# Random features of four strips in one call over four PSUM banks, with all five queues reordered, in a two-layer attention and feed-forward kernel

## What is computed

```python
# 1: linear attention by random features, 16 heads of 8, 32 features, causal
q = x_normed * 128**-0.25;  k = ctx * 128**-0.25
q' = exp(q @ R) + 1e-4
k' = exp(k @ R - 0.5*sum(k*k) - max_over_everything(-0.5*sum(k*k))) + 1e-4
x = x + tanh(g) * (causal sum of q'.k' v) / (causal sum of q'.k')
# 2: token-shifted feed-forward: r = sigmoid(xr @ Wr.T); k = relu(xk @ Wk.T)**2
x = x + tanh(g) * r * (k @ Wv.T)
# 3: attention of ctx (queries) over layernorm(x) (keys, values), softmax twice
a = softmax(q @ k.T * s);  gate = 0.5*mean(g) + 0.5*max(g)   # g = normed @ w_la
a = w * softmax(gate * a) + (1 - w) * a
x = x + tanh(g) * ((a @ v) @ w_proj + b)
# 4: quantized SwiGLU: rows to 8 bits by their largest value, weights to -1, 0, 1
x = x + tanh(g) * bitlinear(silu(bitlinear(x, w_gate)) * bitlinear(x, w_up), w_down)
```

## Time and profile before

| | |
|---|---|
| median of 3 runs | 507.24 us |
| all runs | 501.98, 507.24, 509.07 us |
| the profiled execution | 502.71 us |
| its span, first to last instruction | 501.0 us |
| TensorE matmul busy | 457.8 us (91%) |
| VectorE busy | 412.7 us (82%) |
| ScalarE busy | 367.7 us (73%) |
| GpSimd busy | 303.1 us (60%) |

### The profile page before, as it was taken

How to read it: one execution, slowest core, us unless ns; L and a number is a source line. 1 busy time by engine, 2 the same in 40 slices (tenths; PEclk the granted TensorE clock), 3 DMA queues, 4 the chain that set the end, 5 groups by cost and what they waited for, 6 DMA issues and landing times.

```text
span 501.0 us, 19011 instructions
## 1 busy us (share of the span) xinstructions
PE 457.8 (91%) x7616; PEld 336.0 (67%) x7616; DVE 412.7 (82%) x1374; ACT 367.7 (73%) x774; POOL 303.1 (60%) x416
## 2 busy tenths in 40 slices
PE   6678899999999999999999999999999999876864
PEld 2266568777868686868777777778686868554631
DVE  4752666999989898989898989999998989988734
ACT  4455565979797978797878878797979797776542
POOL 6142357576767585858575776767676758384520
PEclk9996979999999999999999999999999999999888
DMA  6401010101101010101010101010010100000000
GB/s 218 120 4 42 6 40 4 40 7 22 34 13 44 11 48 10 47 9 49 7 50 7 51 6 50 6 29 28 19 39 11 46 11 15 9 15 8 6 12 10
DMA packets 31526, 15.15 MB, mean 30 GB/s; under 512 B 12496, under 2 KB 30800, under 8 KB 31440
## 3 DMA queue, kind: packets, MB, share of 16 engines
q1 hardware_dynamic: 31296, 13.92, 10.4%
q10 hardware_dynamic: 144, 0.02, 0.0%
HBM read 9.73 MB, written 2.10 MB: 24 GB/s over the span
## 4 chain that ended last, share of the span: by engine, by line
PE 67%; DVE 18%; issue 6%; ACT 3%; DMA 2%; SPq 2%; POOL 1%; DVEq 0%
PE MC L1548 13%; PE TP L1513 10%; PE FP L1424 7%; PE MA L1440 6%; PE SP L1504 4%; PE SP L1616 4%; DVE SL L1043 3%; DVE emn L1049 3%; PE FP L1403 2%; PE MA L1469 2%; PE SP L1488 2%; PE FP L1360 2%; PE FP L1407 2%; PE FP L1363 2%; PE FP L1405 2%
## 5 line engine op out<-in xcount | busy, mean ns | idle before, releaser
L1548 PEld LDWEIGHTS MC<-Vc,ET 128*64 128x64 f32 x2048 | 65.0, 138 | 22.1 <-issue 19.4
L1548 PE MATMUL MC<-Vc,ET 128*64 128x25 f32 x2048 | 71.6, 218 | 2.1 <-DVE X L1157 1.2
L413 POOL TENSOR_SCALAR ft<-ft 128x512 f32<-128x512 f32 x64 | 39.7, 620 | 52.2 <-ACT ft L634 48.5
L436 POOL TENSOR_TENSOR Zn<-E,rsh 128x1024 f32<-128x1024 f32 x32 | 60.9, 1904 | 11.4 <-DVE rsh L1057 10.1
L444 POOL TENSOR_TENSOR Zn<-Zn,Gs 128x1024 f32<-128x1024 f32 x32 | 60.9, 1904 | 2.7 <-DVE Gs L1067 2.6
L681 ACT ACTIVATE ET<-TP 128x512 f32<-128x512 f32 x64 | 36.5, 597 | 29.3 <-PE TP L1513 29.3
L997 DVE TENSOR_TENSOR WT<-FP,mask 128x512 f32<-128x512 f32 x64 | 41.9, 676 | 10.2 <-PE FP L1424 10.2
L1037 DVE TENSOR_REDUCE mx<-SP 128x16 f32<-128x1024 f32 x32 | 39.0, 1218 | 4.9 <-PE SP L1504 4.8
L675 ACT ACTIVATE ET<-TP 128x512 f32<-128x512 f32 x64 | 37.6, 587 | 6.8 <-PE TP L1513 5.6
L1513 PE MATMUL TP<-ident,E 128*128 128x128 f32 x256 | 39.7, 289 | 1.1 <-ACT E L670 0.9
L1424 PE MATMUL FP<-ft 32*64 32x64 f32 x2048 | 37.9, 223 | 2.3 <-DVE WT L997 1.9
(11 more groups left out here) (211 smaller groups left out, 1179.1 us busy)
## 6 DMA issues: line engine op xcount, KB each, us to landing
Cd<-in_ctx SPq DMA_DIRECT2D x32, 128.0 KB, 3.0
kX<-kT SPq DMA_DIRECT2D x256, 8.0 KB
X<-in_x SPq DMA_DIRECT2D x16, 128.0 KB, 2.7
call<-in_ctx SPq DMA_DIRECT2D x4, 512.0 KB, 6.5
out_x<-X SPq DMA_DIRECT2D x16, 128.0 KB, 2.1
wffn<-in_L_ffn_w_gate SPq DMA_DIRECT2D x1, 256.0 KB, 4.6
wffn<-in_L_ffn_w_up SPq DMA_DIRECT2D x1, 256.0 KB, 4.9
wffn<-in_L_ffn_w_down SPq DMA_DIRECT2D x1, 256.0 KB, 7.1
```

What stands on the lines that cost most here:

```text
L413: pool.tensor_scalar(f, f, EPS_K, 1.0, ALU.add, ALU.mult).then_inc(s("ftp"), 1)
L436: pool.tensor_tensor(z, E1[u][:, :].rearrange("p (h m) -> p h m", m=64), rsh[u][:, :].unsqueeze(2).to_broadcast([P, H, 64]), ALU.subtract) ...
L1548: last = mm(MC[64 * j:64 * j + 64, c + 32 * q:c + 32 * q + 25], weights[:, q, 64 * j:64 * j + 64], Vc[g.p][:, 2 * u + j, q, 0:25], start=T ...
```

## The change

`features` becomes one call for four strips, over the two banks of FP and the two of SP. It is held until the last `less` of the round's stage c has read the scores, and `ffn_gu`, `rows_CT`, `queries` and `scores`, which use SP, are held until the exponentials have read it. With it the five orders are new, as are the waits that go with them:

```diff
-            def features(g, w):
+            def features(g):
                 at_ends(pe, g, s("WT"), g.k * 4)
-                if w == 0:
-                    at(pe, s("Vc"), g.k * 2)
-                    at(pe, s("csq"), g.k + 1)
-                    at(pe, s("kT"), g.k)
-                    at(pe, s("qcT"), g.k + 1)
-                elif w == 1:
-                    at_ends(pe, g, s("Vc"), g.k * 2)
-                    at_ends(pe, g, s("kT"), g.k)
-                    if not g.first:
-                        at(pe, s("fe"), g.k * 4 + 2)
-                bank = SP_ if g.first and w == 1 else FP
-                strips = [(32 * i, 512 * (i % 2), i) for i in (2 * w, 2 * w + 1)]
-                for r, o, i in strips:
+                at(pe, s("Vc"), g.k * 2)
+                at(pe, s("csq"), g.k + 1)
+                at(pe, s("kT"), g.k)
+                at(pe, s("qcT"), g.k + 1)
+                at(pe, s("ls"), g.k * 2 - 2)
+                strips = [(32 * i, (FP, SP_)[i // 2], 512 * (i % 2), i) for i in range(4)]
+                for r, bank, o, i in strips:
                     mm(bank[:, o:o + 256], Rf[r:r + 32, i, :], qcT[r:r + 32, 0:256], start=True, stop=True)
...
# ScalarE
             def features(g, w):
-                at(act, s("f"), g.k * 2 + 1 + w)
-                f = (SP_ if g.first and w == 1 else FP)[:, :].rearrange("p (i t n) -> p t i n", i=2, t=2)
+                if w == 0:
+                    at(act, s("f"), g.k + 1)
+                f = (FP, SP_)[w][:, :].rearrange("p (i t n) -> p t i n", i=2, t=2)
# VectorE
-                v.tensor_tensor(rsh[u][:, :], emn[u][:, :], pos[g.p][:, u, :], ALU.max).then_inc(s("rsh"), 1)
+                v.scalar_tensor_tensor(rsh[u][:, :], emn[u][:, :], 1.0, pos[g.p][:, u, :], ALU.mult, ALU.max).then_inc(s("rsh"), 1)
-                v.tensor_tensor(Gs[u][:, :], gate[g.p][:, u, :], rs1[u][:, :], ALU.mult).then_inc(s("Gs"), 1)
+                v.scalar_tensor_tensor(Gs[u][:, :], gate[g.p][:, u, :], 1.0, rs1[u][:, :], ALU.mult, ALU.mult).then_inc(s("Gs"), 1)
-                    v.wait_ge(s("css"), i + 1)
-                    v.tensor_reduce(cmins[:, i:i + 1], css[:, H * r:H * r + H * n], op=ALU.min, axis=AX.X)\
-                        .then_inc(s("cmins"), 1)
-                v.wait_ge(s("cmins"), 5)
-                v.tensor_reduce(cmin[:, :], cmins[:, :], op=ALU.min, axis=AX.X).then_inc(s("cmin"), 1)
+                v.wait_ge(s("css"), 5)
+                v.tensor_reduce(cmin[:, :], css[:, :], op=ALU.min, axis=AX.X).then_inc(s("cmin"), 1)
```

More of the change, by code:

```diff
@@ L533, in prepare @@
             def prepare():
-                squares(0)
-                squares(1)
+                for i in range(5):
+                    squares(i)
+                masks()
                 act.wait_ge(s("wv_in"), 32)
@@ L724, in step @@
                 if e:
-                    quant_mul(e)
-                if d:
-                    softmax1(d, 2)
-                if e:
                     ffn_in(e)
-                if b:
-                    if b.first:
-                        round_weights()
-                    gates_Tb(b)
                 if d:
@@ L743, in step @@
                 if c:
+                    if c.first:
+                        weights_turned()
                     yC(c)
+                if d:
+                    softmax2(d, 1)
+                if c:
+                    queries_in(c)
+                if e:
+                    ffn_scale(e, 0)
+                if b:
+                    keys(b)
+                if c:
+                    queries(c)
+                if d:
+                    softmax2(d, 2)
                 if a:
+                    if a.k == 1:
+                        scale_weights()
                     yA(a)
                 if d:
-                    softmax2(d, 2)
-                if c:
-                    queries_in(c)
-                if d:
                     softmax2(d, 3)
-                if b:
-                    keys(b)
                 if e:
-                    ffn_scale(e, 0)
+                    ffn_scale(e, 1)
+                    ffn_mid(e, 0)
                 if a:
@@ L759, in step @@
                 if c:
-                    queries(c)
+                    gates_Tb(c)
+                if b:
+                    values1(b)
+                    if b.first:
+                        round_weights()
+                    yB(b)
                 if a:
                     squares_T(a)
-                if b:
-                    values1(b)
-                if e:
-                    ffn_scale(e, 1)
                 if d:
                     attended(d)
+                if c:
+                    softmax1n(c, 0)
                 if b:
-                    yB(b)
+                    if b.first:
+                        wait_setup()
+                    shift_rows(b)
+                if e:
+                    ffn_mid(e, 1)
+                if c:
+                    softmax1n(c, 1)
                 if a:
                     if a.first:
-                        masks()
                         prepare()
                     features(a, 0)
-                if e:
-                    ffn_mid(e, 0)
-                if b:
-                    shift_rows(b)
-                if c:
-                    softmax1n(c, 0)
-                if a:
                     features(a, 1)
@@ L1266, in step @@
                 if b:
+                    if b.first:
+                        weights_clipped()
                     token_mix(b)
@@ L1645, in step @@
             def step(a, b, c, d, e):
[L1646 to L1649 removed]
                 if d:
+                    if d.k == NG - 1:
+                        warm_end(2)
                     outA(d, 0)
[L1652 to L1657 removed]
                 if e:
@@ L1664, in step @@
                 if b:
-                    out0(b, 0)
+                    if b.first:
+                        weights_total()
+                        warm(2)
+                    if b.k == 1:
+                        warm(2)
+                    weights0(b, 1)
                 if e:
@@ L1684, in step @@
                 if d:
+                    turn2(d, 1)
+                if b:
+                    if b.first:
+                        warm(1)
+                    out0(b, 1)
+                    proj_ctx(b)
+                if c:
+                    rows_CT(c)
+                if d:
                     outB(d, 0)
-                if b:
-                    proj_ctx(b)
+                if c:
+                    queries(c)
                 if d:
@@ L1748, in step @@
                 if c:
+                    gates_bc(c)
                     turn1(c, 1)
+                if b:
+                    if b.first:
+                        weights_turn()
+                    ffn0_in(b)
                 if e:
```

380 lines of the change are left out of this document (184 added, 196 removed).

## The result

The changed kernel takes **551.19 us** (median of 3 runs, 550.53 to 554.79) against 507.24 us before: a ratio of 1.0998, with a 95% interval from 1.0947 to 1.1049. It is slower by ten per cent, where I forecast 498 us, a difference of under two per cent. The profiled execution's span is 548.8 us, 47.8 us over the 501.0 of before.

The account below looks back on a forecast made before the run. TensorE was taken to bound the kernel narrowly, its saving lost to waiting on a loop. Twelve rounds by 0.0, start -4, drain -1: 5 us off 502.71 gives 497.7, forecast 498 us, range 487 to 518.

Parts of the forecast that it names:

- The one call: Features on TensorE: one call of four strips takes 1.5 us instead of two calls' 2.98; bounds 1.5 and 3.0.
- TensorE's work: TensorE's own work per round falls from 26.48 by 1.49 to 24.99 us; alone, twelve rounds would give 18 us.
- The loop of 26.5 us: Round through TensorE, ScalarE's queue, features, GpSimd's constants and weights0: 26.5 us against 26.48, so no gain; kept 25.7 to 26.9.
- whose slack is 2.1: VectorE per round, from busy time: 2.1 us to spare, so Gs waits up to 1.6 us more would partly hide.
- does not wait: Three-operand rsh and Gs on VectorE don't wait for GpSimd; VectorE gains 0.55 us a round, hidden by slack.
- the four Rf: Start of trace: this form, two SBUF inputs, kept pace beside GpSimd's rs_A (0.84 instead of 0.69 us); taken as not waiting.
- Rival 2: rsh and Gs on VectorE wait for GpSimd, delaying the quantiser: 2.0 us a round, 24 us in all, 520 us; chance 0.27.
- The start: Setup to the second group's weights0: 4 us saved with the shorter features, bounds 0 and 6.
- the forecast of 23 us: First masked weights begin at about 23 instead of 27.01 us, through an earlier load and less work behind it.
- The drain: End after the last rounds, without features, quantization moved a round earlier: 1 us saved (-2 to 3).

Follow-up runs that it names:

- pool_mul_start: Changed kernel with rsh (as product and sum) and Gs moved to GpSimd, plus kX cleared early and companion weights scaled and rounded earlier on ScalarE: 511.38 us, 1.0126 of before.
- pool_mul: Changed kernel with both small operations on GpSimd, Gs as a product and rsh as a product and a sum, without start edits: 517.98 us, 1.0207 of before.
- before_start: Kernel before, own loop, with only the change's start moves (later loads, weights sum and weights_mean) and kX cleared early: 502.60 us, 0.9943 of before.
- stt_in_before: Kernel before with rsh and Gs written in the three-operand form, its order and two features calls kept: 505.52 us, 0.987 of before.

## Why the prediction was wrong, by its own steps

**The one call: right. TensorE's work: too low.** The one call took 1.51 us where I took 1.5. TensorE is busy 25.56 us a round against my 24.99. I had also subtracted from the round's length, 26.48. By the busy time of before, 26.19, the fall is 0.63 us (0.93 in pool_mul_start) and not 1.49; where the rest went was not followed.

**The loop of 26.5 us: nearly right in size by luck, wrong in its path.** Without the waits the round is 26.99 us. I closed the loop through features, GpSimd's constants and weights0. In after the chain goes another way: y_D, the quantiser, all of VectorE's queue up to hh, TensorE, and ScalarE back to y_D. I had checked ScalarE and TensorE operation by operation and VectorE only by its sum ("whose slack is 2.1"). With the waits gone (pool_mul_start) the chain of a round runs through TensorE's queue and, ahead of features, through VectorE's largest and less of the last scores:

```profile
277.56 1.24 DVE mx L1046
...
278.81 1.24 DVE SL L1052
```

That is the wait for less(c, 1) that I had named, but not the way through ScalarE, GpSimd's constants and weights0 that I had summed. The difference of 0.5 us a round is 5.4 us over twelve rounds of 26.99 (5.8 measured in pool_mul_start, 6.1 in pool_mul).

**"I take 'does not wait'": the step that failed.** I weighed it against the four Rf at the start, which ran on at their pace beside a GpSimd operation. That comparison could not carry it. The Rf were already running when rs_A began; the one that took longer was rs_A, 0.84 us instead of 0.69, as if they held the resource and it had to wait. The fourth Rf did begin while rs_A ran, at 4.56, and took its 0.28 us. But rs_A is a power of two columns, and the two-operand Gs does not wait for such a power either (the twelve cases above). I compared a new form beside a power with an old form beside a product, and gave to the form what belongs to GpSimd's instruction. The old rsh of 0.71 us waited for a product of 1024 columns, which is what the new places have beside them. What the runs show in place of "does not wait": in after rsh waits up to 1.24 us and Gs 1.60, as long as in the old form, and this is worth 1.91 us a round. The Trainium skill, page "SBUF — State Buffer", section "SBUF: two separate sides", describes an exclusive lock, held for a whole instruction by whichever of the two comes first, and names no form that is exempt. The long operations agree with it: both forms wait, to within 0.04 us of the end of GpSimd's instruction, and an input in PSUM ends the wait. The twelve Gs inside a power of 0.70 us do not agree, and there the measurement decides.

**Rival 2: the right mechanism, a price that came out right in part by luck, and a base that lacked two terms.** I gave 2.0 us a round. Measured, the rounds at full clock are 28.90 us against 26.99 without waits: 1.91. Twelve times that is 22.9 us of the 34.6 in the full rounds. The order is 5.4. The third term was nowhere in my sum: in five rounds the wait for hh let TensorE idle 1.4 us, its granted clock fell, and each took 1.27 us more, 6.3 in all. My reason for the price was wrong all the same (I let the quantiser carry it; see the run with its order changed), so its size is not a result of it.

**The start: the forecast of 23 us right for the path I followed, with two things missed on it.** I took the clearing of kX to lie beside other work. GpSimd's memset held VectorE for 2.83 us, the same lock again, where I had looked for it only in the loop. And I followed the load and VectorE, but not ScalarE's queue, in which the scaling of the weights now stands between keys and y_A (the prediction named only the rounding ahead of the squares, and gave it up to 1 us). Forecast -4, measured +4.9. With both undone and the clock held, the second group's masked weights are 5.2 us ahead of before (43.3 against 48.5), so the gain that I forecast is there, and larger; before_start, which has no other edits, keeps 2.8 of it.

**The drain: wrong.** Forecast -1, measured +6.1, or +5.4 if it is counted from the last group's masked weights: 91.2 us to the end in after, 85.8 before. This stretch differs from trace to trace: 85.8 to 87.2 in the three with the old order, 86.7 to 89.0 in the five of the new order without both waits, 90.8 to 92.1 in the five with both. So about 3 of the 5.4 us go with the waits, and about 1 is left to the new order, which the spread hardly lets one tell. How much of the 3 is the waits and how much the clock was not taken apart.

**The sum of the miss.** I had the span 5 us shorter, and it is 47.8 longer: 52.8 us. Of these the waits in the full rounds are 22.9, the clock 6.3, the order 5.4, the two rounds ahead of them 2.2, the start 8.9 and the drain 7.1. The step that failed explains the largest part, and not all of it; rival 2 alone would have given 520.

**What was not settled:** why an idle stretch of 1.4 us lets the clock fall in some rounds and not in others, and the three late rounds of 29.5 to 30.5 us in the run with the filled stretch.

## What to carry to other kernels

Before you move a small VectorE operation with two SBUF inputs, or GpSimd work beside it, list what GpSimd runs at its new place: beside a long one it ends when that one does, and a 0.16 us operation can cost 1.8. Compare like with like: a short power of two columns held nothing here, and said nothing about a product of 1024 columns. Putting one input in PSUM, or the operation on GpSimd itself, removes the wait; another form of instruction does not. Slack taken from a sum of busy time says nothing when the engine's whole queue lies on the loop, so follow the loop through each engine's queue before you call a wait hidden.

## What the runs showed of the hardware that I had not expected

- A memset on GpSimd, which reads nothing, held a VectorE operation of 2 columns with one SBUF input (mus) for 2.83 us. In the run with both waits gone by place, mus came 0.25 us ahead of the memset and took 0.22 us; there two operations of 128 columns were held, Wqs at 21.53 and bpr at 21.66, the second a successor in the queue. They waited for both memsets together (VectorE's timeline of that run):

```profile
20.62 0.22 DVE L865 TENSOR_SCALAR mus<-mus 128x2 f32<-128x2 f32 x1
...
21.27 0.34 DVE L869 TENSOR_SCALAR WvT<-TP,hB 128x128 f32<-128x128 f32 x1
21.53 2.97 DVE L871 TENSOR_SCALAR Wqs<-wqn 128x128 f32<-128x128 f32 x1
```

  The Trainium skill, same page and section, has the lock also for a fast mode of VectorE that uses both ports. These rows fit it, though no row says in which mode an operation ran. WvT, of the same size with its input in PSUM, ran in 0.34 us beside the same memset.
- A power on GpSimd grows with its columns: 0.70 us for 2 and 2.90 for 16, where a product of 16 takes 0.22.
- Beside GpSimd's power of 2 columns (0.70 us) a VectorE operation with two SBUF inputs runs free: 0.17 to 0.18 us, twelve times in before and twelve in stt_in_before.
- Features in two calls over different row groups and banks overlap across the calls: 2.04 us for what one call does in 1.51.
